# Second attention: the order of a head's loads, the step at which the next head's maxima begin, and the engine that writes the constant row

## What is computed

```python
    x = L0_attn_x
    xn = _layernorm(x, axis=-1)
    x = x + _L0_attn_ref(xn, ...) + _L0_ffn_ref(xn, ...)
    xn = _layernorm(x, axis=-1)
    x = x + _L1_attn_ref(xn, ...) + _L1_ffn_ref(xn, ...)
    return x
...
        qr, kr = (rotate(q), rotate(k))
        scale = HD ** (-0.5)
        scores = jnp.einsum('bhid,bhjd->bhij', qr, kr) * scale
        probs = jax.nn.softmax(scores, axis=-1)
        out = jnp.einsum('bhij,bhjd->bhid', probs, v)
        out = out.transpose(0, 2, 1, 3).reshape(b, n, INNER)
        return out @ w_out + b_out
```

## Time and profile before

| | |
|---|---|
| median of three runs | 3351.94 us |
| the profiled execution | 3346.46 us |
| its span | 3344.7 us |
| mean granted clock of TensorE | 0.881 of full |
| busy share of TensorE, ScalarE, VectorE, GpSimd over the span | 89%, 89%, 83%, 75% |
| the second attention | about 2031 to 3169 us of the span |

### The profile page before, as it was taken

One profiled execution on the slowest core, in us unless ns is written; L12 is line 12 of the kernel. 1 busy time (PEld: TensorE's weight loads), 2 busy tenths in 40 slices (PEclk: granted clock), 3 DMA queues, 4 the chain that ended last, 5 costly groups with the idle time before them and its releaser, 6 DMA issues. The chain is left out here.

```text
span 3344.7 us, 58506 instructions
## 1 busy us (share of the span) xinstructions
PE 2978.6 (89%) x19523; PEld 1261.6 (38%) x19523; DVE 2775.2 (83%) x4212; ACT 2989.8 (89%) x2783; POOL 2504.1 (75%) x1645
## 2 busy tenths in 40 slices
PE   6888888888888888888888796999999999999899
PEld 4222222212221222122211342566656665666548
DVE  7889999999999999999999896877777787778341
ACT  3999999999999999999999684799999999999832
POOL 5888888888888888888868363688688877887650
PEclk9797778877887788778877897999999999999999
DMA  2000000000000000000000264000110011001100
GB/s 71 12 8 8 5 2 7 7 7 0 7 7 7 0 7 7 7 0 7 7 10 1 68 214 115 27 27 27 43 35 27 27 27 51 27 27 27 35 9 14
DMA packets 59509, 85.23 MB, mean 25 GB/s; under 512 B 10064, under 2 KB 45904, under 8 KB 58960
## 3 DMA queue, kind: packets, MB, share of 16 engines
q1 hardware_dynamic: 59344, 82.93, 8.6%
HBM read 52.31 MB, written 30.54 MB: 25 GB/s over the span
## 5 line engine op out<-in xcount | busy, mean ns | idle before, releaser
L1266 POOL TENSOR_TENSOR lo<-pr,hi 128x1024 f16<-128x1024 f32 x384 | 813.0, 2154 | 217.1 <-ACT hi L1445 215.0
L1326 DVE TENSOR_REDUCE mx<-mx_ps 128x1 f32<-128x512 f32 x1024 | 664.1, 686 | 195.3 <-PE mx_ps L1488 190.7
L1461 ACT ACTIVATE pr<-s_ps 128x1024 f32<-128x1024 f32 x512 | 529.1, 1033 | 111.6 <-PE s_ps L1519 105.4
L1445 ACT ACTIVATE hi<-pr 128x1024 f16<-128x1024 f32 x512 | 545.3, 1065 | 0.0
L722 ACT ACTIVATE wt<-wt 128x2048 f32<-128x2048 f32 x256 | 485.2, 1896 | 0.5
L713 ACT ACTIVATE wt<-wt,theta_bias 128x2048 f32<-128x2048 f32 (+2 forms) x160 | 482.3, 3015 | 3.0 <-DVE wt L563 2.5
L501 POOL TENSOR_TENSOR wt<-base,wt 128x1024 f32<-128x1024 f32 x192 | 455.3, 2371 | 16.1
L501 POOL TENSOR_TENSOR wt<-vb,wt 128x1024 f32<-128x1024 f32 x192 | 454.9, 2369 | 16.0
L1538 PE MATMUL pv_ps<-vh,hi 128*128 128x129 f16 x4096 | 425.2, 220 | 11.3 <-POOL lo L1266 5.7
L1538 PE MATMUL pv_ps<-vh,lo 128*128 128x65 f16 x4096 | 411.2, 193 | 0.0
L1488 PE MATMUL mx_ps<-ka,qa 128*128 128x512 f16 x1024 | 360.0, 387 | 54.5 <-DMA ka<-qk 28.4
(11 more groups left out here) (210 smaller groups left out, 5021.7 us busy)
## 6 DMA issues: line engine op xcount, KB each, us to landing
qk<-stg SPq DMA_DIRECT2D x6, 2048.0 KB, 10.8
vh<-v SPq DMA_DIRECT2D x16, 520.0 KB, 3.4
qa<-qk SPq DMA_DIRECT2D x16, 512.0 KB, 3.5
ka<-qk SPq DMA_DIRECT2D x32, 256.0 KB, 4.9
v<-v_st SPq DMA_DIRECT2D x3, 2080.0 KB, 7.9
qst<-parts_dram SPq DMA_DIRECT2D x144, 32.0 KB
kst<-parts_dram SPq DMA_DIRECT2D x144, 32.0 KB
qk<-stg SPq DMA_DIRECT2D x4, 1024.0 KB, 7.9
```

The lines of the kernel that those rows point to most:

```text
L1266: eng.tensor_tensor(lo[:, i % NHL, :, :], pr_slot(i), hi[:, i % NHL, :, :], ALU.subtract).then_inc(lo_done, 1)
L1326: eng.tensor_reduce(mx4[:, q // NCH, q % NCH:q % NCH + 1], mx_ps[:, q % 2, :], AX.X, ALU.max)\
L1445: eng.activation(hi[:, i % NHL, :, :], pr_slot(i), ACT.Copy).then_inc(hi_done, 1)
L1461: eng.activation(pr_slot(i), s_ps[:, i % 2, :, :], ACT.Exp, scale=SM).then_inc(exp_done, 1)
```

## The change

Four edits, all in `stage_attention1`: `MX0` goes from 2 to 3; a head's two `ka` loads are issued ahead of `qa`; the two memsets of the constant row move from VectorE's program to GpSimd's; TensorE waits for them behind the first chunk's maxima instead of ahead of them.

```diff
--- before.py
+++ after.py
@@ -1202,7 +1202,7 @@
     KP = NT // 2
     STEPS = NS * KP
     NMX = NT * NCH
-    MX0, MX1 = 2, STEPS - 5
+    MX0, MX1 = 3, STEPS - 5
     mx_at = [min(NMX, max(0, -(-NMX * (i - MX0) // (MX1 - MX0)))) for i in range(STEPS + 1)]
 
     NQ1 = NMX // NS
@@ -1277,9 +1277,9 @@
 
                     sp.wait_ge(s_done, STEPS * (h + 1))
                     q, k = io["qk1"][0], io["qk1"][1]
-                    for dst, src, sem_ in ((qa[:, par, :], q[h, :, :], loaded),
-                                           (ka[0:HD1, par, :], k[h, 0:HD1, :], loaded),
+                    for dst, src, sem_ in ((ka[0:HD1, par, :], k[h, 0:HD1, :], loaded),
                                            (ka[HD1:P, par, :], k[h, 0:HD1, :], loaded),
+                                           (qa[:, par, :], q[h, :, :], loaded),
                                            (qb[0:HD1, par, :], q[h, 0:HD1, :], rest_loaded),
                                            (kb[0:HD1, par, :], k[h, HD1:P, :], rest_loaded)):
                         sp.dma_start(dst, src).then_inc(sem_, 16)
@@ -1317,10 +1317,6 @@
 
             @block.vector
             def _(eng):
-                for par in range(2):
-                    last = eng.memset(kb[HD1:HD1 + 1, par, :], MROW)
-                last.then_inc(const_ready, 1)
-
                 def reduce_bank(h, q):
                     eng.wait_ge(mx_done, NMX * h + q + 1)
                     eng.tensor_reduce(mx4[:, q // NCH, q % NCH:q % NCH + 1], mx_ps[:, q % 2, :], AX.X, ALU.max)\
@@ -1419,6 +1415,10 @@
 
             @block.gpsimd
             def _(eng):
+                for par in range(2):
+                    last = eng.memset(kb[HD1:HD1 + 1, par, :], MROW)
+                last.then_inc(const_ready, 1)
+
                 def join(h, c):
 
                     eng.wait_ge(sums_taken, NS * h + c + 2)
@@ -1586,10 +1586,10 @@
                 eng.sem_inc(attn_ready, 1)
                 eng.sem_inc(rden_ready, 1)
                 eng.sem_inc(mrow_loaded, 16)
-                eng.wait_ge(const_ready, 1)
                 for q in range(NQ1):
                     mx_bank(0, 0, q)
                 first_turn(0)
+                eng.wait_ge(const_ready, 1)
                 scores(0, 0, 0)
                 one(0, 0, first=True)
                 one(0, 1)
```

## The result

| | before | changed |
|---|---|---|
| median of five runs | 3348.43 us | 3330.06 us |
| lowest and highest | 3344.41 to 3352.87 | 3329.5 to 3335.96 |
| the profiled execution, span | 3346.46, 3344.7 | 3329.5, 3327.7 |
| first to last row write of heads 1 to 15 (14 heads) | 952.45 | 932.47 |

The ratio is 0.9946, 95% interval 0.9935 to 0.9958: 18 us faster. 3329.4 was forecast. With the two further runs the median of before is 3.5 us lower than the one the forecast started from, so the gain is 18.4 against 22.5.

A forecast was written before the change was run, and what follows sets the result against it. TensorE bounds the second attention, ScalarE close behind. 19.7 us from the heads plus 2.8 us from the lower clock make 22.5 us off the 3351.94 us median: 3329.4 us, range 3316 to 3340 (0.75).

The forecast's parts named there:

- The two waits in step 2: At a change of head, TensorE's first bank waits for the load, the next for VectorE's reduce; together 2.0 us per head.
- The arithmetic of the head: Steps 3 and 4 of each head, banks starting at step 3: 1.41 us gained per head, 19.7 us in all.
- The new wait for the copy: In step 4 the weighing waits for ScalarE's copy emptying `pv_ps`: 0.60 us of new waiting per head.
- Rival 1: The copy doesn't hold TensorE in step 4: gain 2.0 us per head, 31 us in all, 3321 us; chance 0.13.
- GpSimd's cover: Slack between GpSimd's last `lo` of a head and TensorE's weighing in step 27: 2.6 us shrinks to 1.2, costing nothing now.
- The denser banks: 64 banks per head in 24 steps instead of 25: the same work on TensorE, no loss.
- The lower clock: Two slow heads, each with an idle stretch of about 2 us, regain 1.4 us each of lower TensorE clock: 2.8 us.
- Rival 2: TensorE's lower clock comes in every head, costing 19.6 us: 3 us of gain left, 3349 us; chance 0.08.
- Keys ahead of queries: At each head's loads, the order frees nothing; the set lands in 6.4 to 7.6 us as now, free up to 8.0.
- The rival that ends slower: Queries placed last land the set after 8.0 us, each further us costing 14; at worst about 3403 us; chance 0.04.
- The estimate from the Trainium skill: A head's load set lands in 5.6 us in either order; the old schedule would have no load wait, that gain nil.
- The constant row: At the stage's start, moving VectorE's two memsets of 1.76 us to GpSimd gains nothing: 0 taken.

The follow-up runs named there:

- Run 1: Only the maxima's first step (`MX0`) goes from 2 to 3, against the kernel before: 3326.74 against 3350.21 us, ratio 0.9931.
- run 2: Only the two `ka` loads go ahead of `qa`, maxima from step 2, against the kernel before: 3362.58 against 3350.21 us, ratio 1.0032.
- run 4: The kernel before, banks still from step 2, but VectorE does the half of `lo` ahead of reduce 0: 3334.04 against 3350.21 us, ratio 0.9943.
- run 5: The kernel before with maxima from step 3 and ScalarE emptying `pv_ps` ahead of exp 4: 3326.38 against 3350.47 us, ratio 0.9921.
- run 3: Only the constant row's memsets go to GpSimd, with TensorE's wait behind the first chunk's maxima, against the kernel before: 3349.29 against 3350.21 us, ratio 0.9997.

## Why the prediction was right, and where not

**The two waits in step 2, and their removal: right.** Run 1 shows that `MX0` alone brings the gain. But I had added the two waits as if each cost its own length. Runs 2 and 4 show that they are one: up to 1.6 us of load wait lay inside the time in which the half of `lo` waited for GpSimd. The sum was nearly right because both went together; a shorter load wait alone brings nothing in a quiet head. This is what the profile of before had in it already: 67.85 us in heads whose load wait was 0.35 and in heads where it was 1.6. A head of that order without any load wait was never seen.

**The arithmetic of the head: right to 0.2 us.** Forecast from scores 3 to the end of step 4: 2702.83 - 2696.13 = 6.70; measured 2693.47 - 2686.67 = 6.80. Bank 0 comes 1.58 after scores 3, forecast 1.57. The missing 0.1 is the copy: it takes 0.68 us here and not the 0.60 of the earlier trace rows, and the weighing starts 0.09 behind it and not 0.05. The gain per head was put at 1.41 and is 1.25. By the end of step 4 it is 1.34 (14.39 us from the first issue before, 13.05 now); from there to the next row write the changed kernel takes 52.09 us in place of 52.02, though the forecast had both the same. The heads were to be 66.4 to 66.6 apart and are 66.60.

**The new wait for the copy: right.** 0.60 forecast, 0.66 measured in the quiet heads; run 5 takes it away and gets 0.63 us per head. Rival 1, under which there is no such wait, fell.

**GpSimd's cover: mis-sized.** 2.6 us were to become 1.2, since the head is 1.4 shorter. But GpSimd, which no longer stands beside the 2.05 us half, finishes earlier too: its last `lo` of a head ended 2750.22 - 2690.32 = 59.90 us after the first issue, and now 58.80. It and the weighing of step 27, in the head that began at 2612.80:

```profile
2668.80 4.26 POOL L1266 TENSOR_TENSOR lo<-pr,hi 128x1024 f16<-128x1024 f32 x2
```

```profile
2675.45 0.22 PE L1538 MATMUL pv_ps<-vh,hi 128*128 128x129 f16 x1
```

2675.45 - 2673.06 = 2.4 us are left. In run 5 waits for `lo` turn up, but on ScalarE and at no cost to the head, so that GpSimd is the next bound isn't shown.

**The denser banks: nearly nothing, as said.** The 0.07 us that a head loses behind step 4 may lie here; no run shows it.

**The lower clock: right.** The two heads of 69.24 and 69.40 us ran at a granted clock of 0.89 over 16 us behind the change of head, where all others stood at 1.00; in the changed kernel all 14 stand at 1.00. Rival 2 didn't come about. In the three profiles with banks from step 2 and reduce 0 ahead of the half (before, runs 2 and 3) 8 of 42 heads have the lower clock, in the seven others none of 98. That it takes one idle stretch of 2 us, as the forecast had it, isn't borne out: in run 3 it fell in a head with waits of 0.22 and 1.81 us, and in run 2 it stayed at 1.00 behind one of 2.45.

**Keys ahead of queries: the step that failed.** I had put the landing at "6.4 to 7.6 as now". In run 2 it is 0.7 us later in the median and up to 8.2, in the changed kernel up to 8.45, and run 2 is 12 us slower on its own, of which the steps of 2.1 us, that I hadn't seen, make 8.3. The rival that ends slower had the right mechanism for the changed kernel, with the right limit (8.0 us from the issue): waits of 0.24 to 0.90 us are left in four of its heads, after loads of 7.8 to 8.5 us, and cost nothing up to 8.00, 0.15 us at 8.22 and 0.38 at 8.45. What saved the forecast is that step 3 gives that much room. The estimate from the Trainium skill ("SBUF — State Buffer", Door 1: the DMA port swizzle) was 5.6 us in either order, with no wait for the loads. The trace doesn't agree: before, the first bank waits for them in all 14 heads (0.32 to 2.10 us), and the orders differ. Why `qa` takes 6.0 us behind the keys, where the keys took 4.9 behind it, wasn't tried.

**The constant row: right.** Run 3 gives 0.9997.

**The sum.** 22.5 forecast. 14 * 1.25 = 17.5, plus 2.9 for the two slow heads, less 0.5 for loads that are still late in two, is 19.9, and the row writes show 20.0; the medians show 18.4. The forecast of 3329.4 lies 0.7 us from the measured 3330.06, and that closeness is luck: the gain was put 4.1 us too high, and the median it was taken from was 3.5 us too high.

## What to carry to other kernels

A bank of work that two engines share must be placed by the latest of its inputs, and what stands behind it in the *other* engine's order has to be looked at too: here the loss of a quiet head was an unrelated half of `lo`, queued behind a reduce that waited. Find the first step at which nothing waits and stop there; one more step cost as much as half the gain. Of the four edits in one change, one carried all, one was harmful alone, and the two for the constant row, tried together, did nothing: test them apart.

## What was not expected

The order of three loads, 1 MB in all, on one queue and into the same places, moves the landing of the set, read as the median distance from the first issue to the first bank: 6.4 us with the 128-partition load first, 7.1 with it last. `ka` lands 4.9 us after its issue behind `qa`, and 3.8 ahead of it; `qa` 3.5 and 6.0.

VectorE's subtraction with both inputs in SBUF ran only where a GpSimd subtraction ended: 0.69 us alone, 2.05 and 2.36 beside one. So a wait for the load of 2.10 us cost nothing by the half and one of 2.17 cost 2.08 us. The Trainium skill ("SBUF — State Buffer", Who interferes with whom) calls it an exclusive lock, held for the whole instruction; the trace agrees, and adds that behind a GpSimd that has work queued the next slot is one of its instructions away.
